# Two halves of a y transform issued in a row, with the next layer's first set of products behind them, in a Fourier layer tower

## The reference, cut to what matters

```
for i in range(L):                                   # L = 4
    x1 = _fourier_layer(v, W1, W2)                   # rfft2, modes x weights, irfft2
    x2 = jnp.einsum('bcxy,cd->bdxy', v, w_w[i]) + w_b[i][None, :, None, None]
    v = x1 + x2
    v = (v - mean) * jax.lax.rsqrt(var + BN_EPS)     # mean, var over batch and positions
    v = v * bn_g[i][None, :, None, None] + bn_b[i][None, :, None, None]
    if i < L - 1:
        v = jax.nn.relu(v)
```

## Time and profile before

| | |
|---|---|
| three runs | 1342.45, 1347.76, 1348.53 us |
| profiled execution, its own time | 1344.41 us |
| its span in the trace | 1342.4 us |
| mean granted clock of TensorE | 0.936 of 2.4 GHz |
| TensorE matmul busy | 1164.1 us (87%) |
| VectorE busy | 849.5 us (63%) |
| ScalarE busy | 555.0 us (41%) |
| L1709 (y transforms), the group that reads only `arena` | 149.8 us for x3072 |
| HBM traffic over the span | 206 GB/s |

### The profile page before, as it was taken

One profiled execution on the slowest core, in us unless ns is written; L12 is line 12 of the kernel. 1 busy time (PEld: TensorE's weight loads), 2 busy tenths in 40 slices (PEclk: granted clock), 3 DMA queues, 4 the chain that ended last, 5 costly groups with the idle time before them and its releaser, 6 DMA issues.

```text
span 1342.4 us, 40668 instructions
## 1 busy us (share of the span) xinstructions
PE 1164.1 (87%) x18235; PEld 665.2 (50%) x18235; DVE 849.5 (63%) x1044; ACT 555.0 (41%) x811; POOL 373.2 (28%) x536
## 2 busy tenths in 40 slices
PE   5898899999989899898998989999889886964696
PEld 4554555555544455454555445555555552324652
DVE  7575676777757567576775756666666571048664
ACT  2165354444546344344444644444434471111150
POOL 8672113224244304031333530222212351110000
PEclk8899899999999999899999998999899988885788
DMA  6578999998328999999963889999998177841001
GB/s 166 142 201 214 273 245 227 216 236 200 98 90 222 234 333 362 345 351 322 343 199 92 202 234 342 349 328 366 321 308 248 29 269 250 352 168 38 1 1 32
DMA packets 156119, 300.29 MB, mean 224 GB/s; under 512 B 33064, under 2 KB 100024, under 8 KB 139012
## 3 DMA queue, kind: packets, MB, share of 16 engines
q1 hardware_dynamic: 131656, 251.53, 61.1%
q0 software_dynamic: 20864, 44.73, 11.9%
q10 hardware_dynamic: 3426, 1.44, 0.4%
HBM read 147.86 MB, written 128.48 MB: 206 GB/s over the span
## 4 chain that ended last, share of the span: by engine, by line
PE 61%; DVE 11%; DMA 10%; ACT 6%; issue 6%; SPq 5%; POOL 1%; DVEq 0%; ACTq 0%; POOLq 0%
PE ps L1647 14%; PE ps L1686 12%; PE ps L1721 7%; PE ps L1709 7%; PE ps L1609 4%; PE ps L1672 3%; PE ps L1573 3%; DMA arena<-maps 3%; DMA maps<-arena 2%; SPq L1171 2%; PE ps L1786 2%; ACT arena L1450 1%; PE ps L1548 1%; PE ps L1588 1%; DMA half_inverse<-arena 1%
## 5 line engine op out<-in xcount | busy, mean ns | idle before, releaser
L1686 PEld LDWEIGHTS ps<-arena 48*128 48x128 f32 x3072 | 187.7, 194 | 91.9 <-issue 86.4
L1686 PE MATMUL ps<-arena 48*128 48x128 f32 x3072 | 207.8, 286 | 12.0 <-issue 6.4
L1450 ACT ACTIVATE arena<-ps,arena 128x1024 f32<-128x1024 f32 x96 | 112.3, 1202 | 225.3 <-PE ps L1686 199.9
L1120 POOL DMA_DIRECT2D arena<-arena x207 | 120.4, 589 | 293.8 <-ACT arena L1467 289.9
L1459 ACT ACTIVATE ps<-ps 128x1024 f32<-128x1024 f32 x144 | 145.5, 1011 | 102.6 <-PE ps L1647 102.5
L2104 DVE STREAM_TRANSPOSE arena<-ps 128x1024 f32<-128x1024 f32 x96 | 177.5, 1932 | 1.2 <-PE ps L1709 1.2
L1647 PE MATMUL ps<-arena 32*32 32x512 f32 x2944 | 152.1, 610 | 10.9 <-DMA arena<-maps 7.5
L2091 DVE STREAM_TRANSPOSE arena<-arena 128x2048 f32<-128x2048 f32 x64 | 144.3, 2289 | 20.6 <-issue 14.2
L1709 PE MATMUL ps<-arena 32*32 32x512 f32 x3072 | 149.8, 604 | 4.6 <-DVE arena L2091 3.4
L1721 PE MATMUL ps<-arena 128*64 128x96 f32 x2304 | 124.5, 260 | 31.3 <-DVE arena L2104 25.7
L1721 PEld LDWEIGHTS ps<-arena 128*64 128x64 f32 x2304 | 105.4, 144 | 81.4 <-issue 45.5
(11 more groups left out here) (321 smaller groups left out, 1438.7 us busy)
## 6 DMA issues: line engine op xcount, KB each, us to landing
arena<-half_inverse SPq DMA_DIRECT2D x90, 384.0 KB, 11.6
half_inverse<-arena SPq DMA_DIRECT2D x120, 256.0 KB, 4.5
maps<-arena SPq DMA_DIRECT2D x112, 256.0 KB, 4.5
maps<-inputs SPq DMA_DIRECT2D x112, 256.0 KB, 12.0
arena<-maps SPq DMA_DIRECT2D x28, 1024.0 KB, 17.4
maps<-arena SPq DMA_DIRECT2D x28, 1024.0 KB, 15.3
inputs<-maps SPq DMA_DIRECT2D x28, 1024.0 KB, 20.6
arena<-in_mode_w POOLq DMA_DIRECT2D x48, 384.0 KB, 7.4
```

The costliest lines, as they stand in the source:

```text
L1120: eng.dma_start(dst, src).then_inc((modes_st[batch % 2], last_st, late_st)[part], 16)
L1450: nc.scalar.activation(half(h_out(l, q), h)[:, 1024 * pair:1024 * pair + 1024], ps[:, 2 * pair:2 * pair + 2, :].rearrange("p b n -> p (b n ...
L1686: last = nc.tensor.matmul(ps[:, b, at:at + 128], gtile[s][rows, 4 * b + 2 * h + n, :], iy[rows, :], start=False, stop=(i >= 2 and n == 1))
```

## The change

`next_set(l, q - 1, 0)` trades places with `y_transform(l, q - 1, 1)` in TensorE's program. No other engine's program changes, and the number of instructions stays the same.

```diff
                     if q:
                         y_transform(l, q - 1, 0)
+                        y_transform(l, q - 1, 1)
                         next_set(l, q - 1, 0)
-                        y_transform(l, q - 1, 1)
                     if q < QUADS:
                         out_set(l, q, 1)
```

## The result

The changed kernel took 1374.41 us (median of 4 runs, 1362.13 to 1386.15), the kernel before 1348.14 us (median of 4, 1342.45 to 1354.42). The ratio is 1.017, with a 95% interval of 1.011 to 1.023: slower by 23 us (15 to 31). One of the four, that of 1386.15 us, counts as slow and is left out of the ratio, which is why the ratio is smaller than 1374.41 / 1348.14. The profiled execution is the one of 1362.13 us, 17.7 more than the profiled one of before, and the fastest of its four. So the trace shows less than the timed runs do.

What follows compares the result with a forecast made beforehand. TensorE's stream, held up by VectorE's statistics and transposes, was taken to set pass 0, engines and transfers in turn the others. 10.4 + 5.9 + 2.7 + 3.2 = 22.2 us, less absorption, gave 19: 1345.8 + 19 = 1365 us, range 1353 to 1376.

Steps and rivals of the forecast that it cites:

- my own case: Whole kernel: slower, 1365 us, own range 1358 to 1371; chance 0.75, including the rival that transfers absorb all (1361).
- The chain of an undisturbed round: out_set(q,0), y transform, next products, statistics, transposes, x transform: statistics 0.69 us later, so the round grows from 15.31 to 16.00.
- the hole 1.16: TensorE, ahead of out_set(q,1): a new hole of about 1.16 us, overlapping the same delay and not added to the price.
- the wait for L2104: TensorE's wait for VectorE's transposes ahead of the x transform, 0.55 us before; forecast to stay near 0.5 us.
- The length of a set, 1.08: Full price of one more set in a row, 1.08 us, read from round 16; 0.69 where it fills the relus' hold.
- The better overlap: Rival, all passes: sets overlap better than in round 16, 0.14 to 0.3 us a round, 1354 us; chance 0.13.
- Pass 0: 15 rounds at 0.69 us each, 10.4 us; its stretch grows from 231.06 to about 241.5 us.
- Round 16: Last round of each pass: nothing covers the moved set, statistics and last x transforms 1.08 us later, 3.2 us for three.
- Passes 1 and 2: 5.9 and 2.7 us, paid mainly in rounds where the x transform waits for VectorE, less what transfers absorb.
- what I had named as a sign of being wrong: Passes 1 and 2 growing by more than pass 0; the forecast had them together grow by less.
- The absorption in pass 2: Rounds waiting for a later load, as round 2 for 1.70 us, swallow earlier losses: all of pass 2 but 1.4 us.
- The clock rival: The new hole lowers the granted clock, 3% or 7 us in pass 0 and some more elsewhere: 1375 us; chance 0.08.

Runs made afterwards that it cites:

- the two parts: New order in pass 0 only, and in passes 1 and 2 only, against the kernel before: 1358.66 us (ratio 1.0087) and 1364.67 us (ratio 1.0134).

## Why the prediction was right, and where it was off

The forecast was slower with 0.86, 1365 us in a range of 1353 to 1376. It came out slower, at 1374.41, inside the range but above the 1358 to 1371 of my own case. Of the 9.4 us between 1365 and 1374.41, 2.3 are the kernel before (1348.14, where I had started from 1345.8). The price itself is 23 us (15 to 31) against 19, and 30 by the two parts. Step by step:

- *The chain of an undisturbed round* was right to the hundredth: statistics 3.28 us after the relu, x transform 8.45 after the y transform against a forecast 8.46, 12 of the 14 rounds of pass 0 within 15.97 to 16.00 against 16.00, the hole 1.16, the wait for L2104 unchanged. That the place of the statistics makes the price was shown by shortening them: the 0.69 fell to 0.03.
- *The length of a set, 1.08*, read from round 16 of before, held: 1.06 there after. Only where the relus had already held the products was it cut to 0.69. The better overlap (0.14 to 0.3 a round) did not come. The 0.92 us that was worked out for it adds 0.06 to a distance from first record to first record, 0.86, that already holds such spacing.
- *Pass 0*: forecast 10.4 for 15 rounds, measured 9.96 for 14, of which 11 paid 0.69 and one, at a lower clock, 2.42. The kernel with pass 0 alone gave 12 us (6 to 17), with its round 16. The stretch from the first relu on grew to 240.24 us and not to 241.5: I had counted 15 rounds in it, and the first of them has no y transform.
- *Round 16*: 1.08 each was right for the statistics. From its y transform to the first filler matmul behind the x transforms it took 12.42, 11.51 and 12.43 us, against 10.80, 10.76 and 10.92, so 1.3 more in the mean: the x transforms took 4.11, 3.18 and 4.11 us and not 3.55, 3.51 and 3.66.
- *Passes 1 and 2* are the term that was mis-sized. I gave them 5.9 + 2.7, took off the middle of what transfers could absorb, 3.3, and added two rounds 16, 2.2: 7.5. The kernel with the new order in these passes alone measured 18 (10 to 26), and the estimate from the profiles at full clock is 0.54 a round, 16 us for 30 rounds. So most of the 20.7 that 30 rounds can pay was paid, also by rounds that I had priced at little or nothing. It is also what I had named as a sign of being wrong, that passes 1 and 2 grow by more than pass 0: by the timed kernels it is 18 against 12, with intervals that overlap, though the profile after shows 2.6 against 10.0.
- *The absorption in pass 2* rested on a misread row. The hole of 1.70 us in round 2 of pass 2 I took for a wait for a load. But the profile puts it down to issue, that is, to nothing that it shows, and it stands within the set, after 7 of its 32 records. The program waits for a load only ahead of the first, and the one other wait within the set, for the statistics, had been met at 824.29 us:

```profile
823.72 1.05 PE L1647 MATMUL ps<-inputs,arena 32*32 32x512 f32 x7
826.47 1.53 PE L1647 MATMUL ps<-inputs,arena 32*32 32x512 f32 x25 [1.70 <-issue]
827.93 3.79 PE L1686 MATMUL ps<-arena 48*128 48x128 f32 x32
```

  The inverse behind it took 3.79 us and not 2.05, at a granted clock of 0.54 (826.47 to 833.84), and the round took 20.00 us. In pass 2 of before no hole of TensorE over 0.3 us is ended by a load (in pass 1 four are, 7.5 us together); the largest group is this, 8 times, 7.7 us:

```profile
PE ps L1647 <- issue: 7.7, 8, 1.7
```

- *The clock rival*: 0.99 in the passes after, against 0.99, 0.98 and 0.96; but 0.96 and 0.96 in the kernel with the new order in passes 1 and 2 only, and 0.95 to 0.99 in the three profiles with the old order. So the new hole of 1.16 us did not lower it in pass 0, and no difference between the orders is seen in the others. For round 16 it was 0.78, 0.91 and 0.76, where it was 0.87, 0.84 and 0.84 before, and 0.86 in pass 0 of the kernel with the new order in round 16 only. That the order lowers it there is not shown.

That the time lies in the range is owed to the right chain in pass 0 and to the width of the range: the term for passes 1 and 2 was less than half of what was measured. What stays open is what ends the holes that the profile puts down to issue, and why passes 1 and 2 pay some 0.5 us a round and not 0.69. Neither leaving out the loads nor issuing them earlier changed the distance between the orders by more than the errors (34 us without, 28 with loads first, 23 with neither).

## What to carry to other kernels

Before moving work ahead in an engine's program, ask which consumer the step that is passed has, and what stands behind that consumer in its own queue: here the early end of the y transform was of no use, because its reader stood behind the statistics, and those became late. Price a moved step by a place in the trace where the same steps stand back to back, less the wait that it now fills. Before a hole is called a wait for a transfer, look at what the profile says ended it, and whether the program has a wait at that place. And a profile of one execution prices only the stretches that repeat to the hundredth; elsewhere, take several, and put the granted clock beside each length.

## What the runs showed of the hardware

Three sets of 16 fp32 products of 32x32 by 512 columns, one on each tile, take 3.42 us when they follow without a wait. The third ends 1.07 to 1.08 us after the second, though the first record of a set follows the first of the set before after 0.86 us and one set alone takes 1.15. The sets overlap only at their edges.

Executions scatter where the order is the same. Pass 2 in the old order took 232.73, 243.08 and 246.06 us, at granted clocks of 0.99, 0.96 and 0.97 and at 313 to 329 GB/s. The 14 rounds of pass 0, at 206 to 218 GB/s, took 215.68, 215.44, 218.51 and 217.97 us in four kernels with the old order there, at a clock of 1.00, and 225.64, 225.60 and 225.61 in three with the new.
